# A graph-attention and expert kernel: GpSimd waits for the last indirect gather of each step before it starts the next step's

## What is computed

```python
xn = _layernorm(x)
# first attention, over all 200,000 edges: h has 4 heads of 64 channels
alpha = leaky_relu(a_src[src] + a_dst[dst])
ex = exp(alpha - amax[dst])
out = segment_sum(h[src] * ex / denom[dst], dst) + bias
x = x + out + mix(xn)
# second attention, the same way over the other 131,072 edges, 4 heads of 4 channels -> scores of 4 experts
g = softmax(top2(mean over heads of layernorm(agg)))
x = x + sum over e of g[e] * (gelu(z @ W1[e] + b1[e]) @ W2[e] + b2[e])
```

## Time and profile before

| | |
|---|---|
| median of the runs | 4169.92 us (3 runs, 4165.97 to 4173.98) |
| the profiled execution, span from first to last instruction | 5269.4 us (no time of its own is listed beside it) |
| busy: PE, DVE, POOL, ACT | 3476.8, 3039.4, 2649.1, 1492.7 us |
| edge stage 1, 143.64 to 3083.40 us of the span | 2939.76 us, 420 steps |
| edge stage 2, 3229.07 to 5125.00 us | 1895.93 us, 265 steps |
| all the rest | 433.71 us |
| gathers in stage 1 and 2 | 1680 and 1060 |

### The profile page before, as it was taken

How to read it: one execution, slowest core, us unless ns; L and a number is a source line. 1 busy time by engine, 2 the same in 40 slices (tenths; PEclk the granted TensorE clock), 3 DMA queues, 4 the chain that set the end, 5 groups by cost and what they waited for, 6 DMA issues and landing times. The chain is left out here.

```text
span 5269.4 us, 87248 instructions
## 1 busy us (share of the span) xinstructions
PE 3476.8 (66%) x16727; PEld 2890.9 (55%) x16728; DVE 3039.4 (58%) x9074; ACT 1492.7 (28%) x4965; POOL 2649.1 (50%) x2767
## 2 busy tenths in 40 slices
PE   5555555665566665666655537888888888888860
PEld 4444444444454444444444436777777777777760
DVE  5566655555565666666666665555555555555558
ACT  3222222222222222222222213333333333333310
POOL 1555555555555555555555522555555555555540
PEclk9777777777777777777777766888888888888865
DMA  5322333332333333333332242111111111111118
GB/s 121 82 78 75 84 82 81 84 84 79 82 82 99 101 101 102 100 101 101 101 84 78 77 79 49 20 20 22 20 20 22 20 20 22 20 21 21 20 16 239
DMA packets 224394, 356.43 MB, mean 68 GB/s; under 512 B 65743, under 2 KB 143761, under 8 KB 224051
## 3 DMA queue, kind: packets, MB, share of 16 engines
q0 software_dynamic: 114560, 234.67, 19.2%
q1 hardware_dynamic: 100624, 109.13, 7.5%
q10 hardware_dynamic: 8867, 9.05, 0.6%
HBM read 294.17 MB, written 45.66 MB: 64 GB/s over the span
## 5 line engine op out<-in xcount | busy, mean ns | idle before, releaser
L791 POOL DMA_INDIRECT msg<-table,idx x1680 | 1630.7, 971 | 1305.1 <-ACT rel L806 844.6
L1466 POOL DMA_INDIRECT xmsg<-xtable,xidx x1060 | 1002.8, 946 | 889.0 <-ACT xidx L1482 589.7
L1159 PE MATMUL psS_e<-msg,hot 128*125 128x260 f32 x3360 | 1182.9, 513 | 281.4 <-issue 162.2
L1159 PEld LDWEIGHTS psS_e<-msg,hot 128*125 128x125 f32 x3360 | 815.5, 254 | 512.3 <-issue 337.3
L888 DVE TENSOR_TENSOR room<-room,psS_e 125x260 f32 x842 | 356.5, 423 | 361.7 <-remote 180.9
L1024 DVE TENSOR_TENSOR msg<-msg,psW_e 128x1024 f32<-128x1024 f32 x420 | 509.5, 1213 | 8.8 <-issue 1.1
L812 ACT CAST hotT<-psT_e 125x512 bf16<-125x512 f32 x422 | 244.7, 580 | 951.6 <-remote 649.7
L1012 DVE TENSOR_REDUCE look<-psD_e 128x32 f32<-128x96 f32 x420 | 106.6, 254 | 700.7 <-remote 553.8
L1076 PE MATMUL psD_e<-ad_b,hotT 125*128 x1684 | 133.9, 182 | 559.8 <-issue 151.3
L1655 PE MATMUL psY<-w,hid 128*125 128x256 f32 x1600 | 457.1, 447 | 56.7 <-issue 29.6
L1065 PEld LDWEIGHTS psT_e<-ident,hot 128*125 128x125 f32 x1692 | 320.7, 240 | 248.2 <-ACT hotT L812 157.7
(11 more groups left out here) (308 smaller groups left out, 4436.9 us busy)
## 6 DMA issues: line engine op xcount, KB each, us to landing
msg<-table,idx POOLq DMA_INDIRECT x1680
experts_out<-y_room SPq DMA_DIRECT2D x101, 224.0 KB
y_back<-experts_out SPq DMA_DIRECT2D x25, 896.0 KB
xmsg<-xtable,xidx POOLq DMA_INDIRECT x1060
xs<-x_all SPq DMA_DIRECT2D x100, 125.0 KB
table<-hrow SPq DMA_DIRECT2D x50, 113.8 KB
x_all<-in_x SPq DMA_DIRECT2D x5, 1120.0 KB
xin<-in_x SPq DMA_DIRECT2D x50, 112.0 KB
```

What stands on the lines that cost most here:

```text
L791: nc.gpsimd.indirect_dma_start(msg[:, u, j, :], None, table[:, :], bass.IndirectOffsetOnAxis(ap=idx[:, u, j:j + 1], axis=0)).then_inc(gath ...
L1159: last = nc.tensor.matmul(psS[:, u % 2, j // GT, 0:ROW], hot[:, u, j, :], msg[:, u, j, :], start=j % GT == 0, stop=j % GT == GT - 1)
L1466: nc.gpsimd.indirect_dma_start(msg[:, u, j, :], None, xtable[:, :], bass.IndirectOffsetOnAxis(ap=idx[:, u, j:j + 1], axis=0)).then_inc(gat ...
```

## The change

After the 4 gathers of a step POOL waits: in stage 1 for the semaphore of the step's fourth gather, in stage 2 for the slot's semaphore at the count at which all 4 have landed. Only then does it go on to the next step. Nothing else is added, removed or moved; the third argument of `gather` only carries the trip's number into the count.

```diff
@@ edges, block.gpsimd
                             nc.gpsimd.indirect_dma_start(
                                 msg[:, u, j, :], None, table[:, :],
                                 bass.IndirectOffsetOnAxis(ap=idx[:, u, j:j + 1], axis=0)).then_inc(gathered[u][j], 16)
+                        pool.wait_ge(gathered[u][ST - 1], s * (TRIPS * 16) + i * 16 + 16)
@@ gating_sums_and_experts, block.gpsimd
-            def gather(k, w):
+            def gather(k, w, visit):
                 u = RING[w % SPAN]
                 pool.wait_ge(staged, k + 1)
                 pool.sem_inc(opened, 1)
...
                         bass.IndirectOffsetOnAxis(ap=idx[:, u, j:j + 1], axis=0)).then_inc(gathered[u], 16)
+                pool.wait_ge(gathered[u], (visit * RING.count(u) + (w // XRING + 1)) * (16 * XT))
 
             with pool.Fori(0, TRIPS) as i:
                 for w in range(SPAN):
-                    gather(i * SPAN + w, w)
+                    gather(i * SPAN + w, w, i)
             for w, k in enumerate(TAIL):
-                gather(k, w)
+                gather(k, w, TRIPS)
```

## The result

The changed kernel takes **5596.16 us** (median of 4 runs, 5594.7 to 5597.95) against 4171.76 us before in the same comparison: a ratio of 1.3411, 95% interval 1.3392 to 1.343. I had forecast 5190 us in a range of 4770 to 5460. The direction and the mechanism are right, the size is 406 us short: the time lies close to my rival "long landing" (5616 us).

What follows compares the result with a forecast made beforehand. Before, POOL's gathers were taken to bound stage 1 and PE stage 2; after, POOL both. 420 steps at 7.08 us (2974), 265 at 6.73 (1783) and 434 us of rest gave 5190 us, range 4770 to 5460.

Steps and rivals of the forecast that it cites:

- long landing: Rival, both stages: landing and restart at their upper bounds, steps of 7.70 and 7.35 us, 5616 us; chance 0.11.
- What bounds the kernel: Before the change, POOL's gather issue sets the pace in stage 1 and PE's busy time that in stage 2.
- POOL's floor: Stage 1 before the change: four gather starts 1.25 us apart, 5.01 us a step.
- the rest: The part of the span that holds no gather, taken as 434 us before and after the change.
- my sum of floors: Whole kernel before: 2104 us stage 1, 1564 stage 2, 434 rest; 4102 us, 68 under the median.
- Landing and issue go in series: POOL's step becomes three starts, landing, then restart: 7.08 us in stage 1, 6.73 in stage 2.
- hidden case: Rival: the wait falls into time POOL spends idle anyway; 4170, at most 4250 us; chance 0.07.
- faster case: Rival: gather issues shorten without earlier gathers in flight; 4077 us with the instruction at 0.45 us; chance 0.02.
- The landing: From the fourth gather's start to its landing: 2.40 to 3.13 us in stage 1, 2.05 to 2.78 in stage 2.
- The restart: From the landing to POOL's next gather start: between 0.30 and 0.81 us, the middle taken.
- The issues: POOL's three starts at 1.25 us in each step, 3.76 us in all.
- The rule of the Trainium skill: Prices a GpSimd DMA at 2.0 us plus bytes at 436 GB/s: landings 2.31 and 2.02 us, 4720 us in all.

Runs made afterwards that it cites:

- e9: The unchanged kernel from before the change, profiled again: a span of 4173.8 us at a run of 4175.7.
- e1: Changed kernel without the wait in stage 2, so the wait stands in stage 1 alone: 5307.71 us, ratio 1.2709.
- e2: Changed kernel without the wait in stage 1, so the wait stands in stage 2 alone: 4476.66 us, ratio 1.0725.
- e3: Changed kernel with POOL waiting, after its four gathers, for the previous step's landing, in 575 of 685 steps: 4175.84 us, ratio 1.0002.
- e4: Changed kernel with the wait in stage 1 alone, for the step's third gather instead of the fourth: 4735.6 us, ratio 1.1338.
- e7: Changed kernel with the wait in stage 1 alone, for the step's second gather instead of the fourth: 4267.06 us, ratio 1.0232.
- e6: Changed kernel, stage 1 alone, POOL waiting for its fourth gather instruction to be done instead of the landing: 4444.0 us, ratio 1.0651.
- e8: Changed kernel with 12 steps instead of 6 in a turn of POOL's stage 1 loop: 5592.78 us, ratio 1.3398.
- e5: Changed kernel, both waits kept, with SP's loads of `xs`, `xin` and `hin` moved only in part: 5561.02 us, ratio 1.3324.

## Why the prediction was wrong in size

- **What bounds the kernel: right.** From a profile stretched by 26% I took POOL's floor of 5.01 us a step in stage 1 and PE's 1564 us in stage 2. Stage 1 runs at 5.16 us a step, stage 2 takes 1594 us, and the rest 414 (I had 434). That my sum of floors came within 70 us of the median is partly luck: PE's 1564 us were read at a granted clock of 0.83. In e9, at 0.89, PE is busy 1448 us in stage 2, and the same sum is 2104 + 1448 + 414 = 3966 us, 206 short.
- **Landing and issue go in series, POOL is the bound in both stages, nothing hides it: right**, shown by e1 to e4 and e7. The trace of the changed kernel shows it step by step too: in stage 1, in slots 0 to 4, the next step's first gather always starts 0.88 to 0.91 us after the semaphore's last update, however late that is. In stage 2 it is 0.85 us, and 1.1 where the loop turns. The hidden case, which took the stretched pace of 7.0 us at its word, and the faster case are refuted.
- **The landing: right.** The middle of my bounds, 2.77 us, is the median landing of 2.8; in stage 2 2.42 against 2.4.
- **The restart: the step that failed.** I set it between 0.30 and 0.81 us and took the middle, 0.55, because "neither is nearer". In e6 it is seen alone: 0.89 us from the end of the awaited instruction to the next start in quiet steps, and in the changed kernel 0.88 us from landing to the next start, above even my upper bound. The 0.81 of the earlier trace rows was the row for this very thing, POOL starting after a wait for somebody else; the 0.30 of a gap between two queued gathers was not. The records of POOL's two small instructions between steps show why. In the changed kernel they end 0.12 us after the landing, and the gather starts 0.76 us behind them; behind ACT's `rel` in the trace of before it is the same 0.76 us. In a step of e3 they ended 0.57 us before the gather in front did, and the gap stayed 0.30 us: there the 0.76 us run beside that gather. 0.34 us in 420 steps are 143 us. In stage 2 the quiet time from the fourth start to the next is 3.24 us, not 2.97: 72 us.
- **Late steps: a term that was missing.** I read the landing where little else moved. Once it is in series, every late one counts: the mean from the fourth start to the next start is 3.95 us in stage 1 against 3.66 in quiet steps, 122 us; in stage 2 3.31 against 3.24, 18 us. Of the 122 us some 95 are landings (3.01 us on the mean, 2.78 in quiet steps) and 28 the turn of POOL's loop (0.41 us in 69 turns, shown by e8). e5 shows SP's transfers as a cause of late landings (46 us in the mix part, 35 in the time). What delays the rest stays open.
- **The issues** take 3.86 us from the first to the fourth start, not 3.76, since some gathers take 1.2 us and more (89 of the 1680): 42 us. In stage 2 3.81, 12 us. Before the change the same gathers are long too, so this was in its 5.16 already.

These terms make 307 us in stage 1 and 102 in stage 2. Stage 1 measured 3288 against my 2974 (+314), stage 2 1889 against 1783 (+106), the rest 416 against 434 (-18): together 402, of the 403 by which the span exceeds 5190. The end at which I arrived is that of "long landing", but by another division of the sum: that rival had a landing of 3.13 us, which did not come, and no late landings.

What the prediction said of the profile after holds: three starts at 1.25 us, the landing as releaser (named in 350 steps of stage 1 and 240 of stage 2; in the step behind a turn of POOL's loop the view says "issue"), DVE's wait at `look` turned to the landing (1347.3 us, 415 times), ACT's `rel` no longer among POOL's releasers. The gap ahead of the first gather is 2.6 us or more, where I had written 2, and the shortest steps take 7.4 us, not 7.1. The profiled span grew by 324 us, less than the runs, as I had written, but for another reason: the stretch of the first profile did not come again.

The rule of the Trainium skill (DMA: Bandwidth & Descriptors, section "Anatomy of one DMA — SWDGE (gpsimd) path") gave estimates of 2.31 and 2.02 us for a gather from issue to landing. The runs show 2.8 and 2.4, so the measurement stands over the page by 0.5 and 0.4 us for these gathers of 128 rows, and the sum made with it (4720 us) was the furthest off of those that keep the series.

No version here beats the kernel before; e3 only equals it. Where an order is needed only one step later, e3's wait, one step behind, had it at no cost.

## What to carry to other kernels

A wait on an engine's own DMA at the end of a step puts the whole landing and the engine's restart (2.8 + 0.9 us here) behind the issues, in every step, if that engine sets the pace; the same wait one step later cost nothing here. Take the restart from a row in which that engine really woke from a wait, not from the gap between two instructions that were queued. And when a latency comes into series, its late cases count too: take the mean over busy stretches, not a quiet moment.

## What was not expected of the hardware

- The profile of before was 1100 us longer than its runs, with irregular stalls on all engines, and a second profile of the same kernel was not. POOL's floor, worked out from starts, held up against it (5.01 us a step for 5.16), the pace of its steps did not (7.00), and PE's busy times were longer in it, at a lower granted clock.
- TensorE's granted clock fell with the pace. The mean in stage 1 was 0.88 of full speed in e9 and 0.70 in the changed kernel, that is, more of the time at the 1.2 GHz level and less at 2.4 GHz, while PE had longer idle times between its steps (638 us in all in e9, 1187 us in the changed kernel); PE's busy time for the same matmuls rose from 1527 to 2102 us. No cost of it is seen in the time: POOL's starts followed the landings alone.
- A gather costs POOL 1.25 us from start to start whether its 128 rows have 1040 or 80 bytes; only the landing differs, by 0.4 us.
